# A graph network layer on one core: the edge loop with cross-term variances, fp32 edge products in 32-row strips and a ring of four halves

## The reference, cut to what matters

```python
n = jnp.maximum(_layernorm(x, axis=-1), 0.0)
row, col = (edge_index[0], edge_index[1])
msg_in = jnp.concatenate([n[row], edge_attr], axis=-1)
h = msg_in @ W1 + b1                      # 160 -> 256 per edge
h = gelu(_layernorm(h, g1, be1))
msg = h @ W2 + b2
agg = segment_sum(msg, col, num_segments=x.shape[0])
u = concatenate([n, agg], axis=-1) @ Wu + bu
u = gelu(_layernorm(u, gu, beu))
x = x + u + n
```

## Time and profile before

| | us |
|---|---|
| runs: median of 3 (lowest, highest) | 4982.13 (4980.34, 4989.26) |
| profiled execution: span from its first to its last instruction | 5038.3 |
| busy in it: TensorE / VectorE / ScalarE / GpSimd | 3638.0 / 2939.9 / 2492.2 / 3210.0 |

### The profile page before, as it was taken

How to read it: one execution, slowest core, us unless ns; L and a number is a source line. 1 busy time by engine, 2 the same in 40 slices (tenths; PEclk the granted TensorE clock), 3 DMA queues, 4 the chain that set the end, 5 groups by cost and what they waited for, 6 DMA issues and landing times. The chain is left out here.

```text
span 5038.3 us, 84982 instructions
## 1 busy us (share of the span) xinstructions
PE 3638.0 (72%) x16168; PEld 2611.6 (52%) x16168; DVE 2939.9 (58%) x8166; ACT 2492.2 (49%) x7380; POOL 3210.0 (64%) x2574
## 2 busy tenths in 40 slices
PE   3438999999999999999999997567633336666600
PEld 1216666666666666666666665565523324444300
DVE  6776776777777777767667775556811113323237
ACT  2437777777777777777777774462200001222200
POOL 2337777777777777777777774102366656888842
PEclk8665555555555555555555555555555555555555
DMA  6964444444444444444444442003311114555558
GB/s 249 343 242 113 117 117 112 115 114 114 117 112 116 113 116 115 114 114 115 111 112 113 116 113 61 12 15 95 101 49 47 44 38 80 75 74 78 74 124 222
DMA packets 726546, 557.03 MB, mean 111 GB/s; under 512 B 278174, under 2 KB 657170, under 8 KB 724594
## 3 DMA queue, kind: packets, MB, share of 16 engines
q0 software_dynamic: 135328, 250.63, 21.7%
q1 hardware_dynamic: 585138, 305.55, 21.4%
q10 hardware_dynamic: 6048, 0.52, 0.1%
HBM read 420.83 MB, written 135.45 MB: 110 GB/s over the span
## 5 line engine op out<-in xcount | busy, mean ns | idle before, releaser
L561 POOL DMA_INDIRECT stage<-p_tab,indices x1568 | 1761.6, 1123 | 660.3 <-issue 468.6
L674 ACT ACTIVATE table_weights_and_bias<-stage 128x256 bf16<-128x256 f32 x1568 | 632.4, 404 | 369.1 <-DVE stage L752 202.1
L768 DVE SCALAR_TENSOR_TENSOR stage<-stage,rstd,g 128x256 f32<-128x256 f32 x1568 | 653.9, 480 | 213.1 <-POOL rstd L567 213.1
L601 PE MATMUL ps_tiles<-edge_weights_a,edge_features_a 128*128 128x256 bf16 x1568 | 611.9, 390 | 201.1 <-DVE stage L752 156.4
L623 PE MATMUL ps_b<-window_mask,stage 128*128 128x32 f32 x3136 | 725.2, 402 | 2.9 <-ACT stage L680 2.9
L623 PEld LDWEIGHTS ps_b<-window_mask,stage 128*128 128x128 f32 x3136 | 698.3, 327 | 46.2 <-issue 43.3
L623 PE MATMUL ps_a<-window_mask,stage 128*128 128x32 f32 x3136 | 718.7, 400 | 1.9 <-ACT stage L680 1.7
L623 PEld LDWEIGHTS ps_a<-window_mask,stage 128*128 128x128 f32 x3136 | 706.8, 330 | 2.5 <-ACT stage L680 2.4
L602 PE MATMUL ps_tiles<-edge_weights_b,edge_features_b 64*128 64x256 bf16 x1568 | 614.4, 392 | 0.0
L752 DVE TENSOR_TENSOR stage<-ps_tiles,stage 128x512 f32<-128x512 f32 x784 | 538.1, 687 | 104.6 <-issue 101.2
L680 ACT ACTIVATE stage<-stage 128x1024 f32<-128x1024 f32 x392 | 414.2, 1057 | 366.8 <-DVE stage L774 332.5
(11 more groups left out here) (258 smaller groups left out, 5413.2 us busy)
## 6 DMA issues: line engine op xcount, KB each, us to landing
edge_features_a<-ea_part SPq DMA_DIRECT2D x784, 64.0 KB
ea_part<-sums SPq DMA_DIRECT2D x42, 896.0 KB, 5.5
sums<-ea_d SPq DMA_DIRECT2D x14, 1792.0 KB, 9.2
stage<-p_tab,indices POOLq DMA_INDIRECT x1568
edge_features_b<-ea_part SPq DMA_DIRECT2D x392, 64.0 KB
acc<-zeros_bf SPq DMA_DIRECT2D x392, 64.0 KB
sums<-acc SPq DMA_DIRECT2D x56, 448.0 KB
sums<-src_d SPq DMA_DIRECT2D x46, 512.0 KB
```

The source lines that it names most:

```text
L561: gp.indirect_dma_start(out=rows[:, j, :], out_offset=None, in_=k.p_tab[:, :], in_offset=bass.IndirectOffsetOnAxis(ap=k.meta[h][:, j:j + 1 ...
L601: nc.tensor.matmul(psH[q][:, t, :], k.eaA[h][:, e:e + P], k.wA[:, :], start=True, stop=False)
L674: nc.scalar.activation(k.scratch[:, j % GROUP, :], z[h][:, j, :], ACT.Square, scale=HID ** -0.5, accum_out=k.ssq[i][:, at:at + 1]).then_in ...
L768: o(v.scalar_tensor_tensor(z[h][:, j, :], z[h][:, j, :], root, k.g1[:, :], ALU.mult, ALU.mult))
```

## The change

The edge loop is rewritten, and what feeds it and takes from it with it.

- **Variance.** With z = p + e W (p the gathered row, e the 32 features), the mean square of z is (p.p)/256 + e.(2pW'/256 + G e), G = WW'/256. `node_tables` now stores with each row of `p_tab` the 32 numbers 2pW'/256 (32 more columns of the product) and p.p/256 (ScalarE, square and accumulate), and multiplies p by g1. A row is 292 numbers wide. In the edge loop TensorE computes G e (2 fp32 matmuls of 128 columns per half, `feature_products`), VectorE adds, multiplies and reduces 32 numbers per edge.
- **Root.** VectorE computes it, by a first guess on the bits and three Newton steps of three operations on 128x8 numbers, spread between the rows of the half before; GpSimd issues only gathers.
- **Edge products.** The features, scaled by the root, are turned by TensorE (2 fp32 transposes per half), copied by ScalarE, and multiplied by W g1 in fp32 with 32 rows, four tiles in the four 32-row strips of the array and in four PSUM banks; be1 is added by a bf16 matmul with 3 rows in each strip.
- **One VectorE pass per row:** row times root plus product (`hidden`, 8 of them) in place of addition, scaling and shift.
- **Windows.** As before two fp32 matmuls per tile; the counts come from 8 bf16 matmuls of one column, and go into a matrix of degrees by one 98-column matmul per half (`window_counts`), with two masks on VectorE. SBUF sums have two blocks of 12544 columns in place of three.
- **Ring.** Gathered rows, indices and features have four buffers each; rows are rewritten in place, and a buffer is free when its windows are summed.
- **Elsewhere.** `node_tables` splits no features any more (features are loaded as they are, 256 KB per half). `node_update` adds counts times b2 on GpSimd in place of the third matmul. `setup_phase` and `far_messages` compute what the new form needs.

The core of the diff, in the edge loop:

```diff
@@ edge_messages, TensorE @@
-                for t in range(2):
-                    e = (2 * q + t) * P
-                    nc.tensor.matmul(psH[q][:, t, :], k.eaA[h][:, e:e + P], k.wA[:, :], start=True, stop=False)
-                    nc.tensor.matmul(psH[q][:, t, :], k.eaB[h][:, e:e + P], k.wB[:, :], start=False,
-                                     stop=True).then_inc(s_tile, 1)
+            def feature_part(H, h):
+                if not inside(H):
+                    return
+                pe.wait_ge(s_ct, H + 1)
+                if from_first(H, 1):
+                    pe.wait_ge(s_f, 2 * H)
+                for g in range(QUADS):
+                    for i in range(GROUP):
+                        part = slice(DE * i, DE * (i + 1))
+                        nc.tensor.matmul(psE[i][:, g, :], k.easT[h][part, g, :], k.w1bg[part, :], start=True,
+                                         stop=False)
+                    for i in range(GROUP):
+                        part = slice(DE * i, DE * i + 3)
+                        last = nc.tensor.matmul(psE[i][:, g, :], k.ones_bf[part, :], k.bep[part, :], start=False,
+                                                stop=True)
+                last.then_inc(s_e, 1)
...
+            def slot(b, r):
+                H = RING * b + r
+                h, o = r % 2, 1 - r % 2
+                turn(H, h)
+                histogram(H - 1, o)
+                feature_part(H, h)
+                window_sums(H - 1, o, (r - 1) % RING)
+                window_counts(H - 2, h)
+                feature_products(H + 2, b + (r + 2) // RING, (r + 2) % RING)
@@ edge_messages, GpSimd @@
-            def rstd(unit, i):
-                gp.wait_ge(s_var, unit + 1)
-                gp.tensor_tensor(k.rstd[i][:, :], k.var[i][:, :], k.neghalf[:, 0:HALF], ALU.pow)\
-                  .then_inc(s_rstd, 1)
...
+                if from_first(b, 1):
+                    wait_apart(k, gp, s_seg, RING * b + r - 3)
@@ edge_messages, VectorE @@
+                done = v.scalar_tensor_tensor(z, z, k.rstd[r % 2][:, j:j + 1], psE[j % GROUP][:, j // GROUP, :],
+                                              ALU.mult, ALU.add)
```

More of the change, by code:

```diff
@@ new lines, in _ @@
+            o(v.tensor_copy(lane_f, lane))
+            o.wait()
+            for q in range(4):
+                rows = slice(WIN * q, WIN * (q + 1))
+                o(v.tensor_scalar(ids[rows, :], k.firsts[rows, q:PAIRS:4], lane_f[rows, :], None, ALU.add))
+            o.wait()
+            o(v.tensor_scalar(id_low, ids, P - 1, None, ALU.bitwise_and))
+            o(v.tensor_scalar(id_high, ids, P.bit_length() - 1, None, ALU.logical_shift_right))
+            o.wait()
+            o(v.tensor_copy(k.id_lo[:, :], id_low))
@@ L305, in node_tables @@
     rstd = [take(NG) for _ in range(2)]
[L306 to L311 removed]
+    squares = [take(HID) for _ in range(2)]
+    assert at[0] <= UCOLS
     psT = [k.psA, k.psB]
@@ L645, in _ @@
-            nc.tensor.matmul(psC, k.zerob[:, :], k.zerob[:, 0:NT], start=True, stop=False)
-            for q in range(PH):
-                product(0, 0, q, True)
-            for h in range(2):
-                slot(0, h, True)
-            with pe.Fori(1, BODIES - 1) as b:
-                for h in range(2):
-                    slot(b, h, False)
-            for h in range(2):
-                slot(BODIES - 1, h, False, ahead=h == 0)
-            window_sums(2 * (HALVES - 2) + 1, 0, 1, False)
@@ L662, in _ @@
+            slot(-1, 3)
+            for r in range(RING):
+                slot(0, r)
+            with pe.Fori(1, LAST) as b:
+                for r in range(RING):
+                    slot(b, r)
+            for r in range(RING):
+                slot(LAST, r)
+            slot(LAST + 1, 0)
+            slot(LAST + 1, 1)
+            nc.tensor.matmul(k.psC[:, 0:2 * NT], k.zerob[:, 0:P], k.zerob[:, 0:2 * NT], start=False, stop=True)\
+              .then_inc(s_hist, 1)
         @block.scalar
@@ L718, in _, with slot @@
[L718 to L724 removed]
+            def slot(b, r):
+                H = RING * b + r
+                h, o = r % 2, 1 - r % 2
+                gelu(H - 1, (r - 1) % RING, 1)
+                take_turned(H, h)
+                far_masks(H, h)
+                masks(H, h)
+                gelu(H, r, 0)
@@ L861, in _ @@
+            v.memset(k.U[:, 0:UCOLS], 0.0).then_inc(s_u0, 1)
+            v.wait_ge(s_u0, 1)
+            slot(-1, 3)
+            for r in range(RING):
+                slot(0, r)
+            with v.Fori(1, LAST) as b:
+                for r in range(RING):
+                    slot(b, r)
+            for r in range(RING):
+                slot(LAST, r)
+            slot(LAST + 1, 0)
+            slot(LAST + 1, 1)
+            v.wait_ge(s_keep, 5 * HALVES)
             v.wait_ge(s_hist, HALVES + 1)
@@ new lines, in _ @@
+        @block.gpsimd
+        def _(gp):
+            n_pairs, _ = trips(gp)
+            gp.iota(columns, [[1, FAR_COLS]], base=1, channel_multiplier=0,
+                    allow_small_or_imprecise_dtypes=True).then_inc(s_i, 1)
+            with gp.Fori(0, n_pairs) as b:
+                for i in range(2):
+                    wait_apart(k, gp, s_ld, loads * (2 * b + i) + loads)
+                    gp.indirect_dma_start(out=rows, out_offset=None, in_=k.p_tab[:, :],
+                                          in_offset=bass.IndirectOffsetOnAxis(ap=src, axis=0)).then_inc(s_g, 16)
+                    gp.wait_ge(s_var, 2 * b + i + 1)
+                    gp.tensor_tensor(rstd, var, k.neghalf[:, 0:1], ALU.pow).then_inc(s_rs, 1)
@@ L1232, in _ @@
             pe.sem_inc(s_mu, 2)
-            for t in range(HT):
-                last = nc.tensor.matmul(psD[:, t:t + 1], k.U[0:1, 2 * UCOLS + t * P:2 * UCOLS + (t + 1) * P],
-                                        k.ones[0:1, 0:1], start=True, stop=True)
-            last.then_inc(s_cnt, 1)
             with pe.Fori(0, n_bodies) as b:
```

1081 lines of the change are left out of this document (623 added, 458 removed).

## The result

The changed kernel took 5470.7 us (median of 4 runs, 5463 to 5476) and the kernel before 4981.2 (4979 to 4989): 1.098 times the time, 95% interval 1.096 to 1.100. The prediction had slower as the likelier side, and 5215 us, with 5300 as the upper end of its range. So the side was right, and the size lay outside the range; that the side was right is luck, since what made the kernel slow is not in the prediction (see "Why the prediction was wrong").

A forecast was written before the change was run, and what follows sets the result against it. TensorE (12.9 us of a 13.9 us half) and GpSimd (13.1) were taken to stand nearly at the bound. 5038 + 333 (edge loop) - 100 (other stages) = 5271 us profiled, 56 lower for the median: 5215, range 4430 to 5300.

The forecast's parts named there:

- GpSimd after: Edge loop: without the power, eight gathers take 11.4 us; GpSimd could do a half in 11.6, no longer first in line.
- F: Edge loop, TensorE: unknown time per half of strip products and shifts, bounded by 2.4 and 9.7 us, taken as 5.2.
- the stagger: Strip products: each strip starts only with the second record of the strip before; F 5.2 us, half 15.6; chance 0.38.
- rival 1: Strip products run together: F 2.4 to 2.5 us, half 12.9, loop -196 us, 4686 us in all; chance 0.22.
- no overlap: Strip products run one after another: F 9.7 us, half 20.1, +1215 us, 6097 us in all; chance 0.13.
- Rival 2: Strip products bound by fp32 loads in a row: F 3.9 us, half 14.3, +78 us, 4960 in all; chance 0.14.
- The rest of TensorE's half: Edge loop: TensorE's work apart from F, from transposes to windows, strip changes and waits, summed to 10.4 us a half.
- rival 3: Edge loop: wide fp32 lifts TensorE's clock, GpSimd's 11.6 us then bounds the half; -451 us, 4431 in all; chance 0.12.
- Other stages: Outside the edge loop: `node_tables` -88 us, setup +4, `far_messages` +5, `node_update` -21; together -100 us.
- The cover of the Newton chain: Edge loop, VectorE: the root's steps lie between `hidden` rows and cost nothing, unless TensorE's half falls under 11 us.
- the 5215: Whole kernel: forecast median in us, from 5038 + 333 - 100 = 5271 for the profiled execution and 56 less for the runs.
- the chance of 0.42 for faster: Whole kernel: 0.22 for rival 1, 0.12 for rival 3, 0.08 of Rival 2's case; slower had 0.53, same 0.05.

The follow-up runs named there:

- full_height: The changed kernel without row strips: fp32 products over 128 rows against zero-padded weights, shift from one strip; 4472.3 us, 0.934 of the kernel before (4790 us).
- after_again: The changed kernel unaltered, run again beside the kernel before on a chip where that took 4790 us; 4368.4 us, 0.912.
- before_unrolled: The kernel before with TensorE's edge loop written out four times, eight halves in the loop body for two; 4787.5 us, 0.999 of the kernel before.
- paced: The changed kernel with an 80-column GpSimd addition between two gathers; 4488.4 us, 0.937 (kernel before 4789 us); repeated where that took 4918 us: 4770.8 us, 0.970.
- shift32: The changed kernel with the shift matmuls over all 32 rows of each strip for three; 4359.2 us, 0.910 of the kernel before (4790 us).
- full_height_3: The full_height kernel run again on a chip where the kernel before took 4918 us; 5372.8 us, 1.093.

## Why the prediction was wrong

**The step that failed** is "GpSimd after": "With four buffers a gather waits for nothing near. So GpSimd could do 11.6, and is no longer first in line." On a free chip the first half is nearly true (GpSimd waits 124.7/88 = 1.4 us a half for window sums), and its work is smaller than the 11.4 of my sum: eight gathers 1.25 us apart, 10.0, since a gather takes 0.955 us for the 1.125 that I carried over. (The step from 11.4 to 11.6 in that passage has no term.) Eight gathers now start in a row, 1.27 us apart here (1512.10 to 1521.01), where before one started every 1000/575 = 1.74 us, with a power of 1.68 us and waits between, and a half took 13.1 us. I counted this as slack. On a held chip it is what holds TensorE: 16.9 us a half (3311/196) for 11.6 on a free one (2270/196), 1041 us in all. I priced gathers by GpSimd's time and the DMA share of 0.43, and gave them no effect on another engine; none of my rivals had one.

**F, the products in strips.** I took the stagger, 5.2 us, because fp32 matmuls have two records each. That was wrong: F is 2.43 us at a clock of 0.50 (the mean of 1511 to 1515.5), rival 1's lower bound. The mark that I named for it, four L683 at nearly the same time, is in the trace: from 1513.36 the first records of four tiles start 0.007 us apart, and 0.59 us after the first record come the second records of all four, as close. So the two records of an fp32 matmul don't stagger the strips. The Trainium skill's 3.07 for four strips (TensorE: Matmul & The Clock Gate, "Measured speedup vs the span model") would have given 3.2; against my 9.7 of no overlap it is 9.7/2.43 = 4.0. But that 9.7 was too high as well: in full_height, without strips, records of 256 columns follow each other at 0.43 us at a clock of 0.50 and not at 0.50 us, which makes an estimated 16 x 0.43 + 8 x 0.21 = 8.6, and 3.5 times. (Rival 2's F, 3.4 and 0.4 for shifts, adds up to 3.8 and not to 3.9.)

**The rest of TensorE's half** was well priced and a little too high. At 1.2 GHz: transposes 0.43 (0.5), histogram 0.79 (0.63), one-column matmuls 0.15 (0.5), windows 6.85 (6.8), feature products 0.98 (1.2), counts 0.07 (0.1). With F that is 11.7 us, where rival 1 had 12.9. So rival 1's mechanism is what free chips show, and its gain is larger: the loop 2270.6 us for 2580.1, -310 for -196, and the kernel 4368 for 4790.

**The clock (rival 3)** rose for part of the loop, to a mean of 0.56 from 0.50. In after_again the window sums of 1510.27 run in 4.87 us where the same 32 take 7.03 at 1.2 GHz; the clock had risen behind the strips, to a mean of 0.78 from 1509 to 1515 us. Over its loop they take 532.3/87.6 = 6.1 us a half for 6.85, so a little of rival 3 is in the gain as well. In the half of the result that is shown it was no help: on the held chip the rise, a mean of 0.70 from 1515.5 to 1524 us, fell into the time in which TensorE stood still.

**Other stages.** `node_tables` -100 (forecast -88, ends -40 and -130): its group now steps by 12.2 to 12.9 us for 20.5, where I had 13.7. Two starts of its new g1 pass on the timeline of DVE:

```profile
120.37 2.02 DVE L434 TENSOR_TENSOR sums<-sums,g 128x1792 f32<-128x1792 f32 x1
...
133.25 2.02 DVE L434 TENSOR_TENSOR sums<-sums,g 128x1792 f32<-128x1792 f32 x1
```

Setup +5 (+4). `node_update` -5 (-21), the one furthest from its forecast. Together about -100, as forecast. The cover of the Newton chain held: in after_again VectorE's idle time before its steps (L874, L880, L887) is 0.0 us of 1000, and before the scaled features behind them 3.0.

**So the 5215** had two errors of opposite sign: a half of 15.6 us where TensorE needs 11.7, and no term for the hold, 5.3 us a half. That "slower" came true is luck: the reason given for it, the stagger, is not there. On a free chip the chance of 0.42 for faster would have been the side that came.

**What stays open.** What the gathers and TensorE share. In the trace of a held chip most of the gathers' landing signals aren't recorded (542 of 1920 for the first of the four buffers between 1000 and 2000 us, 16 for each gather; in after_again 2762 of 2816), and TensorE's own signal `s_e` comes late although its matmuls were issued. In the kernel before it is the same: 3780 of 9200 on the held chip, 9706 of 9840 in before_unrolled on a free one; so the gaps mark the chip, with or without a hold. This fits a path for signals or for records that is full, and so does the count of records at which the hold begins; but these are observations and no test. Each time on record comes with a granted clock, so no run without recording is among them, and whether the recording has a part in the hold is open. Whether bytes written, row size or the number of gathers decide was tried on free chips only.

No version that ran on both kinds is best on both. paced is faster than the kernel before on both kinds (0.937 and 0.970), and than the changed kernel on held chips (1.094 to 1.098); on free chips the changed kernel itself is the fastest that computes the whole result (0.912; shift32 doesn't differ from it).

## What to carry to other kernels

A queue that is relieved of its waits may harm another engine: when a change lets GpSimd issue indirect DMAs back to back, ask what they do to TensorE, and try a short pause between them. Run the unchanged pair, before and after, on the same chip as every experiment; here the sign of the result turned with the chip, and a group without its control seemed to confirm everything. When an engine waits and its releaser was issued long ago, look at what else is in flight over exactly that time, and count records as well as us up to where the wait begins.

## What the hardware showed that was not expected

Matmuls in four row strips run side by side, in fp32 too: 16 records of 32x256 and their 8 bf16 shifts in 2.43 us, four records starting 0.007 us apart. One program took 5469 us on one chip and 4368 on another, 25% apart, with each time repeated within 0.3%, and `node_tables` alike to 1 us. On held chips, gathers that start every 1.48 us and not every 1.25 took the ratio to the kernel before to 0.970, from 1.094 on another held chip and from 1.093 for full_height_3 on the same one; a gate in the middle of the eight gathers did the same, beside 1.094 on the same chip. The hold began after 48 to 52 of TensorE's records, be it 4.7 or 8.8 us after the first gather.
